# TensorE waits for all four banks of a layer's mixing products before the first of them

## The reference, cut to what matters

```python
xxx = x + sx * p['x_maa']
mix = jnp.tanh(xxx @ p['tm_w1']).reshape(b * t, 5, E)             # E = 32
mix = jnp.einsum('nfe,fed->fnd', mix, p['tm_w2'])                 # five products, 32 rows deep
mw, mk, mv, mr, mg = mix
wx = x + sx * (p['w_maa'] + mw)      # the same for kx, vx, rx, gx
```

## Time and profile before

| what | value |
|---|---|
| median of 3 runs | 2980.02 us (2975.94 to 2981.84) |
| the profiled execution's own time | 2979.97 us |
| its span, first to last instruction | 2978.2 us |
| busy: PE / PEld / DVE / ACT / POOL | 92% / 73% / 81% / 50% / 44% |
| mean granted TensorE clock | 0.975 |

### The profile page before, as it was taken

One profiled execution on the slowest core, in us unless ns is written; L12 is line 12 of the kernel. 1 busy time (PEld: TensorE's weight loads), 2 busy tenths in 40 slices (PEclk: granted clock), 3 DMA queues, 4 the chain that ended last, 5 costly groups with the idle time before them and its releaser, 6 DMA issues.

```text
span 2978.2 us, 79496 instructions
## 1 busy us (share of the span) xinstructions
PE 2745.6 (92%) x32829; PEld 2179.4 (73%) x32829; DVE 2420.0 (81%) x5345; ACT 1494.8 (50%) x3155; POOL 1297.6 (44%) x1457
## 2 busy tenths in 40 slices
PE   4779999999999999999999999999999999999875
PEld 3567777777787777777777777777777777777753
DVE  5657888888888888888888888888888888888754
ACT  2445455554545555555555555455555555555331
POOL 3344444444444444444444544444454444444310
PEclk7889999999999999999999999999999999999987
DMA  4000000000000000000000000000000000000000
GB/s 150 14 5 9 13 9 8 9 12 12 12 13 12 5 9 13 12 12 13 12 5 9 12 12 12 13 12 5 9 12 12 12 13 12 5 9 12 8 8 7
DMA packets 36838, 41.56 MB, mean 14 GB/s; under 512 B 3273, under 2 KB 35201, under 8 KB 36481
## 3 DMA queue, kind: packets, MB, share of 16 engines
q1 hardware_dynamic: 35696, 36.32, 3.9%
q10 hardware_dynamic: 784, 0.16, 0.0%
HBM read 28.08 MB, written 8.39 MB: 12 GB/s over the span
## 4 chain that ended last, share of the span: by engine, by line
PE 58%; DVE 24%; ACT 8%; issue 7%; POOL 3%; ACTq 0%; DVEq 0%; DMA 0%; POOLq 0%
PE ps_all L1512 9%; PE ps_all L1545 8%; PE ps_all L1526 7%; PE ps_all L1327 7%; PE ps_all L1563 5%; PE ps_all L1311 3%; PE ps_all L1357 3%; PE ps_all L1430 3%; ACT mixin L941 3%; DVE ffn_work L603 3%; DVE mixin L1120 3%; DVE stats L1053 2%; DVE ffn_work L605 2%; ACT mixin L938 2%; DVE att L1170 2%
## 5 line engine op out<-in xcount | busy, mean ns | idle before, releaser
L770 POOL TENSOR_TENSOR mixin<-mixin,hT_tm 128x512 f32<-128x512 f32 x320 | 402.1, 1273 | 355.1 <-DVE mixin L1120 355.1
L1512 PE MATMUL ps_all<-chan,cwk 128*128 128x256 f32 x1536 | 385.9, 395 | 11.9 <-DVE chan L1099 9.6
L1526 PE MATMUL ps_all<-cwv,chan 128*128 128x256 f32 x1536 | 346.8, 382 | 0.4 <-issue 0.4
L1512 PEld LDWEIGHTS ps_all<-chan,cwk 128*128 128x128 f32 x1536 | 280.3, 192 | 76.0 <-issue 33.3
L911 ACT ACTIVATE chan<-ps_all 128x512 f32<-128x512 f32 x192 | 114.7, 598 | 421.5 <-PE ps_all L1512 419.5
L1526 PEld LDWEIGHTS ps_all<-cwv,chan 128*128 128x128 f32 x1536 | 288.0, 191 | 46.9 <-issue 9.9
L750 POOL TENSOR_TENSOR rstd<-var,powc 128x2 f32<-128x2 f32 x224 | 179.3, 800 | 278.7 <-DVE var L1059 278.0
L1120 DVE SCALAR_TENSOR_TENSOR mixin<-ps_all,vcol,sxrk 128x256 f32<-128x256 f32 x640 | 270.1, 475 | 23.3 <-PE ps_all L1357 13.2
L1170 DVE COPY_PREDICATED att<-masks,ps_all 128x256 f32<-128x256 uint8 x384 | 203.9, 531 | 20.4
L938 ACT ACTIVATE mixin<-ps_all,vcol 64x256 f32<-64x256 f32 x128 | 71.8, 561 | 276.5 <-PE ps_all L1311 275.7
L799 POOL TENSOR_TENSOR mixin<-mixin,bonus 128x512 f32<-128x512 f32 x64 | 83.1, 1298 | 253.2 <-ACT mixin L941 253.2
(11 more groups left out here) (190 smaller groups left out, 6744.3 us busy)
## 6 DMA issues: line engine op xcount, KB each, us to landing
xin<-in_L_attn_x_dram SPq DMA_DIRECT2D x32, 256.0 KB, 2.7
tok<-in_L_attn_x_dram SPq DMA_DIRECT2D x32, 256.0 KB, 2.7
out_dram<-x SPq DMA_DIRECT2D x32, 256.0 KB, 2.1
cwk<-in_L_attn_cWk_dram SPq DMA_DIRECT2D x2, 768.0 KB, 8.0
cwv<-in_L_attn_cWv_dram SPq DMA_DIRECT2D x2, 768.0 KB, 10.1
ffn_work<-in_L_wmod_dram SPq DMA_DIRECT2D x2, 512.0 KB, 5.0
tok<-in_L_ffn_w_down_dram SPq DMA_DIRECT2D x1, 704.0 KB, 4.3
tok<-in_L_ffn_w_gate_dram SPq DMA_DIRECT2D x1, 640.0 KB, 8.8
```

The lines of the kernel that those rows point to most:

```text
L770: pool.tensor_tensor(m, m, hT["tm", l][:, :, :, 1:P + 1].rearrange("p k c t -> p (k c) t"), ALU.add).then_inc(ev["mixed"][b], 1)
L1512: ins = pe.matmul(bank(b, "ck", lj, "k")[:, m * TT:(m + 1) * TT], cwk[:, l, k, n:n + P], k_in[:, k, :], start=(k == 0), stop=(k == KC - 1))
L1526: ins = pe.matmul(bank(b, "cv", l, "v")[:, c * D:(c + 1) * D], relu[t // 2][:, t % 2, c * P:(c + 1) * P], cwv[:, l, t, :], start=(t == 0), ...
```

## The change

Ahead of the program a table `MIXING` is built from TensorE's order: each unbroken run of `mf` stages of the same tile and stream is listed under its first stage. In `mf`, the first stage of such a run now waits for the banks of all stages of the run, and the others wait for nothing of their own. The wait for the first tanh stays where it is. Order, products, banks and all other engines are the same.

```diff
+    MIXING = {}
+    run = None
+    for i, b, kind, arg in RUN[PE]:
+        if kind != "mf":
+            run = None
+            continue
+        if run is None or run[:2] != (i, b):
+            run = (i, b, kind, arg)
+            MIXING[run] = []
+        MIXING[run].append((i, b, kind, arg, "m"))
+
...
             def mf(i, b, lf):
                 l, f = lf
-                fill(pe, i, b, "mf", lf, "m")
+                for use in MIXING.get((i, b, "mf", lf), []):
+                    fill(pe, *use)
                 if f == 0:
                     after(pe, i, "tanh", b, "mix", l)
```

## The result

The median is 2985.77 us (2984.49 to 2988.32, 7 runs) against 2977.89 us (2975.49 to 2981.84, 7 runs) of the kernel before, run in turn with it: 7.9 us more, a ratio of 1.0027 with a 95% interval of 1.0015 to 1.0039. So the change makes the kernel slower by about 0.27%. The time lies in the forecast range, and above the forecast 2983.1. The profiled execution took 2988.32 us, its span is 2986.6 us.

A forecast was written before the change was run, and what follows sets the result against it. TensorE and VectorE were taken to bound the kernel together, handing work to and fro. 24 steady groups at 0.13 us gave 3.1 us, head and tail zero: 2979.97 + 3.1 = 2983.1 us, range 2977.0 to 2989.5.

The forecast's parts named there:

- What holds the group: Stream 0's mf group: bank 7, freed by VectorE line 1196 at 1574.55, comes last of its waits, in 25 groups.
- The price of the release: From bank 7's release to stream 0's first mf product: 0.14 us, making the next step 0.13 us later a group.
- the value from above: Stream 0's mf groups: 0.22 us each if bank 7 stands in the first of two waiting instructions.
- The term of 3.1 us: Stream 0's 24 steady mf groups, counted in full at 0.13 us each.
- the slower rival: Uncovered standing waits ahead of all mf groups: 10.1 us more, 2990.1 us; chance 0.15.
- Head and tail: Ten mf groups at the program's start and end: counted at zero because of idle time; in full another 1.2 us.
- Stream 1 and the other runs at zero: The other 39 mf runs, mostly stream 1: extra standing instruction covered by work in flight, zero; uncovered, 2.7 us.
- Who waits for the three later banks: VectorE, reading mf's banks after the group: 1.2 us of cover, so their later filling costs nothing.
- Absorbed: VectorE holds the path and TensorE's idle 3 us a tile hides the mf delay: 2980 us; chance 0.20.
- Standing waits not covered: All mf groups pay for waits ahead of the load, bank 7 in the first of two: 2990.1 us; chance 0.15.
- The clock: The new TensorE pause brings half clock to the following cv, 28 us in 25 tiles: 3008 us; chance 0.04.
- The overlap gives time back: Stream 0's four mf stages run at once from today's start, 15.8 us less: 2964 us; chance 0.03.

The follow-up runs named there:

- the banks exchanged: Banks of so's two state products swapped: kernel before 2966.66 us (ratio 0.9957), kernel after 2970.93 us (0.9975), against the kernel before at 2979.04 us.
- The first experiment: The changed kernel with its four bank waits in the opposite order, so the load carries bank 7: 2979.3 us, ratio 1.0001 to the kernel before.
- the last run: The changed kernel with the state products' banks swapped and the last stage's bank waited for first: 2965.53 us, ratio 0.9953 to the kernel before.

## Why the prediction came out as it did

**What holds the group: right.** The prediction read from the rows that bank 7, behind `ov` and line 1196, is the last of the five waits in stream 0, 25 times, that four stages together take 1.17 us, and that `cv` follows 1.09 us behind the first product. All of it stands in the rows of after: 25 waits, 1.17 us, 1928.42 - 1927.33 = 1.09.

**The price of the release: the step that failed.** The text gave three values: 0.05 us where the load carries the wait, 0.14 where it stands last ahead of the load, 0.23 where another instruction follows. It took the middle one, "because the waits stand in the code's order and bank 7 is next to last, with the tanh, in the second instruction". The views of lines 551 and 536 show the two in the other order, and the release takes 0.25 to 0.27 us. So the value from above was the true one, 0.22 as priced there and 0.25 as measured, and the middle one was a choice by the code and not by a row. The mechanism stood, and this term of the sum was too small by half. What could have been read beforehand is only that none of the rows I had shown a group with several standing instructions that are really waited for; a term like that deserves its upper value as often as its middle one. The term of 3.1 us, for 24 groups, came to 24 x 0.25 = 6.0. The measured time lies in the range of the prediction only because that range reached up to the slower rival; the most likely outcome by its chances, a time within 6.0 us of the kernel before (0.77), did not come, though the interval still reaches down to 4.5 us.

**Head and tail: open.** The nine groups released by their tanh were counted at zero since over a quarter of the time there is idle. The tail row shows 0.18 us a group at the next step, where the prediction's full price was 0.10 to 0.12, too small for the same reason as above. Whether it reaches the end is not settled, and no run did head and tail alone. For it: 6.2 us alone would leave 1.7 of the 7.9 us without a place. The two profiled executions agree: `cv` of the last steady group begins at 2355.56 us before and at 2362.84 after, 7.3 us later, of which 2.2 us were there at the first group already (193.95 and 196.15), and the spans differ by 8.4 us, so 3.3 of these arise outside. Against it: in the run of stream 1 alone that first `cv` begins at 196.41, as late, with stream 0 unchanged, so a single execution's head proves little; and with the banks exchanged the change costs 4.3 us, less than its 25 groups alone would make.

**Stream 1 and the other runs at zero: right.** The timeline has no gap, and the run of stream 1 alone measured 1.0002 [0.9994, 1.0011], which agrees.

**Who waits for the three later banks: right.** In the tile of 1580 us the four banks are full at 1580.05 + 1.17 = 1581.22, and VectorE reads the first of them here, with no idle time before it:

```profile
1582.28 2.43 DVE L1131 SCALAR_TENSOR_TENSOR mixin<-ps_all,vcol,sxrk 128x256 f32<-128x256 f32 x6
```

That is 1.06 us of cover. The first experiment, which keeps the hold and drops the price of its release, shows the same in the time.

**Absorbed (0.20): fell.** 0.25 us later at line 1369 is 0.25 us more in a tile. **Standing waits not covered (0.15): half right.** Its order of the two instructions and nearly its 0.22 us were what happened, and its part for all other groups (2.7 us) was not, by the rows of stream 1; so the time fell between it and the forecast, past the bound of 6.0 us for "slower", to which 0.20 had been given. **The clock (0.04): fell.** The granted clock is 1.00 from 300 to 2780 us, with a pause of 0.85 us in every tile. The Trainium skill, page "TensorE: Matmul & The Clock Gate", section "A second HAM failure mode: psum-queue depth-cycling", warns of small pauses between groups of matmuls; by that rule, this trace and that of the first experiment (granted clock 1.00 from 300 to 2780 us, pauses of 0.64 us) do not agree at pauses of this size. **The overlap gives time back (0.03): not by the change.** The reason against it, bank 7's release, was the right one: taking that away gives 12.4 us in the kernel before, without the change. The four stages in their row groups do run at once, 16 products in 1.17 us against 1.13 for the four of one stage, as the Trainium skill says on the page "TensorEngine Tiling (Array Packing)", section "Key Properties".

## What to carry to other kernels

When waits are drawn together ahead of one TensorE instruction, find out which comes last and write that one first, so that the load carries it; here this alone gave back the 7.9 us, as far as the noise lets one see. A hold that waits for what ends last anyway cost nothing that could be measured, even though it left TensorE idle for 0.6 us a tile, because the stages behind it run at once. And before moving a wait for a late bank, ask who holds the bank: giving it to a product that is emptied earlier was worth 12.4 us, more than any place of the wait.

## What the runs showed of the hardware

The time from the release of a semaphore to TensorE's first product depends on how the wait is held: 0.04 to 0.05 us when the load carries it (the first experiment), 0.10 to 0.14 us when it stands in the last instruction ahead of the load (the last run, and the earlier trace rows), 0.21 to 0.27 us when one more standing instruction follows, 0.31 us when two follow. Most are listed at 51 ns. While TensorE has work queued they cost nothing, up to the number that the change has in stream 1; with two more the group came 0.11 us later.

A matmul carries the first wait written. The others stand two to an instruction, but not in the order of the code. By the semaphores that the traces name, the groups read here pair them from the middle outwards: written as B, C, 7, tanh behind the carried A, they stand as (C, 7) and then (B, tanh); with four more behind the tanh, as (tanh, fifth), (7, sixth), (C, seventh), (B, eighth). So the second wait of the code stands nearest to the load, together with the last one. This is read from the groups of this kernel, and no run was made to test it as a rule.

A standing instruction's listed time need not show its wait. With bank 7 as the first of its two semaphores it is listed from the release on, at 51 ns; with the late one as the second, the wait is in its length: 702 ns for bank 7 in the run with more standing instructions, 547 ns for bank C in the kernel after with the banks exchanged.
